# Scan of a state-space layer: making the next time steps one tile earlier, in another PSUM bank

## The reference

```python
dt = jax.nn.softplus(ts @ W_dt.T + b_dt)          # time steps, 1024 channels
A = -jnp.exp(A_log.astype(jnp.float32))
def step(state, inp):
    dt_t, B_t, C_t, u_t = inp
    dA = jnp.exp(dt_t[..., None] * A)             # 16 decays per channel
    state = state * dA + (dt_t * u_t)[..., None] * B_t[:, None, :]
    y = jnp.einsum('bdn,bn->bd', state, C_t)
    return (state, y)
...
y = ys.transpose(1, 0, 2) + x * D
```

## Time and profile before

| | us |
|---|---|
| median of 3 runs (range) | 3067.13 (3065.42 to 3069.26) |
| the profiled execution | 3064.25 |
| its span, first to last instruction | 3062.5 |
| busy PE / DVE / ACT / POOL | 2417.9 / 2037.0 / 1590.3 / 1155.5 |
| the scan of batch element 0, about | 619 to 1000 |
| the scan of batch element 1, about | 1153 to 1534 |

### The profile page before, as it was taken

The page is one execution under the profiler, slowest core; times in us unless marked ns, Lnnn a source line. Parts: engine busy times, 40 slices in busy tenths (PEclk is TensorE's granted clock), DMA queues, the critical chain, the costliest instruction groups (busy, mean ns, idle before and its releaser), DMA issues.

```text
span 3062.5 us, 36612 instructions
## 1 busy us (share of the span) xinstructions
PE 2417.9 (79%) x12216; PEld 1889.0 (62%) x12216; DVE 2037.0 (67%) x3145; ACT 1590.3 (52%) x3315; POOL 1155.5 (38%) x1016
## 2 busy tenths in 40 slices
PE   6986989768778866777889889998799998952058
PEld 4344347557667655766767678886578877842046
DVE  3834742578778457877853477885578785498884
ACT  1541640277666127766611166664276664699701
POOL 3011046142123521212356546665456764510071
PEclk9887899778889977888999999999899999965579
DMA  6123223020100120010022211111111111200011
GB/s 214 44 84 97 43 66 90 16 71 14 56 21 25 52 65 22 15 56 22 25 64 88 76 28 53 52 53 52 49 32 52 56 49 56 73 28 0 0 32 45
DMA packets 87842, 155.73 MB, mean 51 GB/s; under 512 B 8840, under 2 KB 17672, under 8 KB 87528
## 3 DMA queue, kind: packets, MB, share of 16 engines
q1 hardware_dynamic: 87656, 153.38, 16.9%
HBM read 138.21 MB, written 14.75 MB: 50 GB/s over the span
## 4 chain that ended last, share of the span: by engine, by line
PE 51%; ACT 15%; DVE 15%; issue 7%; POOL 3%; DVEq 0%; ACTq 0%; POOLq 0%
PE ps L651 45%; ACT tables L1343 5%; PE ps L665 5%; ACT m L1218 3%; DVE f_lo L1382 2%; DVE m_front L1503 1%; PE ps L790 1%; POOL w_lo L595 1%; ACT tables L1182 1%; ACT m L1192 1%; DVE f_hi L1381 1%; ACT L1218 1%; DVE loose L1485 1%; DVE stat L1397 1%; DVE m L1582 1%
## 5 line engine op out<-in xcount | busy, mean ns | idle before, releaser
L594 POOL TENSOR_SCALAR w_hi<-w_in 128x512 fp32r<-128x512 f32 x430 | 315.2, 733 | 1382.4 <-PE ps L651 802.9
L595 POOL TENSOR_TENSOR w_lo<-w_in,w_hi 128x512 fp32r<-128x512 f32 x430 | 624.7, 1453 | 35.9
L651 PE MATMUL ps<-m,tables 128*128 128x128 f32 x2048 | 301.4, 297 | 136.6 <-ACT tables L1182 135.4
L651 PE MATMUL ps<-hT_hi,w_lo 128*128 128x512 f32 x864 | 355.5, 411 | 28.5 <-DVE a L1427 11.7
L651 PEld LDWEIGHTS ps<-m,tables 128*128 128x128 f32 x2048 | 273.6, 209 | 156.0 <-issue 131.0
L651 PE MATMUL ps<-hT_hi,w_hi 128*128 128x512 f32 x864 | 342.6, 397 | 0.0
L651 PE MATMUL ps<-hT_lo,w_hi 128*128 128x512 f32 x864 | 342.2, 396 | 0.0
L1582 DVE TENSOR_TENSOR_SCAN m<-m,m 128x1028 f32<-128x1028 f32 x128 | 308.0, 2406 | 10.0 <-ACT m L1218 4.3
L1218 ACT ACTIVATE m<-m_rows,negA 128x256 f32<-128x256 f32 x512 | 217.3, 498 | 22.2 <-DVE m L1536 15.5
L1554 DVE TENSOR_TENSOR m<-m,m 128x1024 f32<-128x1024 f32 x128 | 177.6, 1388 | 55.3 <-PE ps L665 39.0
L665 PE MATMUL ps<-tables,m 128*128 128x128 f32 x1024 | 164.4, 292 | 63.1 <-DVE m L1582 39.7
(11 more groups left out here) (245 smaller groups left out, 5308.6 us busy)
## 6 DMA issues: line engine op xcount, KB each, us to landing
w_in<-units SPq DMA_DIRECT2D x430, 256.0 KB, 2.6
stack_scratch<-a SPq DMA_DIRECT2D x48, 256.0 KB
a<-stack_scratch SPq DMA_DIRECT2D x64, 192.0 KB, 4.4
m<-bc_scratch SPq DMA_DIRECT2D x16, 512.0 KB, 5.4
out<-x_sb SPq DMA_DIRECT2D x2, 1024.0 KB, 4.3
tables<-small SPq DMA_DIRECT2D x1, 1143.0 KB, 9.9
x_sb<-x SPq DMA_DIRECT2D x4, 256.0 KB, 3.6
x_sb<-x SPq DMA_DIRECT2D x1, 1024.0 KB, 7.6
```

Of the source, the lines that this page charges most:

```text
L594: c["did"](nc.gpsimd.tensor_scalar(w_hi[:, r], raw, 1.0, 1.0, ALU.mult, ALU.mult), s["unit_hi"])
L595: c["did"](nc.gpsimd.tensor_tensor(w_lo[:, r], raw, w_hi[:, r].bitcast(F32), ALU.subtract), s["unit_split"])
L651: ins = T.matmul(out, lhsT, rhs, start=start, stop=stop)
```

## The change

It does two things in the scan.

1. The time steps of tiles i + 2 and i + 3 (i even) are now started in tile i: PE makes the product ahead of the second group of the even tile, in **bank 4**, which it shares with the feed-forward's gate and projection; ACT takes Abs, Relu and Exp at the end of the even tile's second half, and Ln after the first group of the odd tile; DVE's three pieces come before the second, third and fourth group of the odd tile. The semaphore `m_dtx` now tells ACT that the steps are ready, and is raised before the product with the input.
2. The helper `at_ends` is removed, and the feed-forward parts are placed by `mix`, which puts part k after half tile number n when (n + 1) * 30 // 32 passes k.

```diff
-    def at_ends(scans, parts):
-        ...
-            want = (2 * tile + last + 1) * len(parts) // (2 * ends) if last else done + (...) // 2
-    ... + at_ends(scan(0), ffn(1, 4)[3:])
+    ... + mix(scan(0), ffn(1, 4)[3:])
-    ... + at_ends(scan(1), ffn(0, 4)[3:])
+    ... + mix(scan(1), ffn(0, 4)[3:])
@@ PE
                 def time_steps(i):
-                    o, tokens = claim(6, s["m_dt_clip"]), (half + i // DT) * HL
+                    o, tokens = claim(4, s["m_dt_clip"]), (half + i // DT) * HL
-                if q == 0 and i % 2 and (half, i) != (1, DT - 1):
-                    time_steps(i + 1)
                 for g in range(q * QS // NG, (q + 1) * QS // NG):
                     n = scan_group(b, half, i, g)
+                    if g == 1 and i % 2 == 0 and (half, i) != (1, DT - 2):
+                        time_steps(i + 2)
                     states_turned(n, 0)
@@ ACT
-                        go(A(m_e[:, r], ps[:, 6, r * HL:(r + 1) * HL], ACT.Abs, bias=bias))
+                        go(A(m_e[:, r], ps[:, 4, r * HL:(r + 1) * HL], ACT.Abs, bias=bias))
                     ...
                     did(A(m_e, m_e, ACT.Exp, scale=-1.0), s["m_dt_exp"])
+
+                def time_steps_ln():
                     did(A(m_l, m_e, ACT.Ln, bias=1.0), s["m_dt_ln"])
...
                         states_kept(n - 2, 1)
+                    if g == 0 and i % 2 and (half, i) != (1, DT - 1):
+                        time_steps_ln()
-                if q == 0 and i % 2 and (half, i) != (1, DT - 1):
-                    time_steps(i + 1)
+                if q == 1 and i % 2 == 0 and (half, i) != (1, DT - 2):
+                    time_steps(i + 2)
@@ DVE
-                    did(V.tensor_tensor(dt, dt, m_v, ALU.add))
+                    did(V.tensor_tensor(dt, dt, m_v, ALU.add), s["m_dtx"])
+
+                def time_inputs(i):
...
-                    if q == 1 and i % 2 and (half, i) != (1, DT - 1):
-                        if g == QS // NG:
+                    if i % 2 and (half, i) != (1, DT - 1):
+                        if g == 1:
                             time_steps_1(i + 1)
-                        else:
+                        elif g == 2:
                             time_steps_2(i + 1)
+                        elif g == 3:
+                            time_inputs(i + 1)
```

More of the change, by code:

```diff
@@ L131, in schedule @@
     s += flat(ffn(0)[:3]) + [("attn_out", 1), ("ln_rows", 1), ("fgate", 0, 1, 5), ("fproj", 0, 1, 5), ("fmul", 0, 1, 5), ("ln_turn", 1), ("fdown", 0, 0)]
-    s += flat(ffn(0)[6:]) + flat(ffn(1)[:2]) + ln(0) + flat(ffn(1)[2:3]) + front(0) + at_ends(scan(0), ffn(1, 4)[3:])
+    s += flat(ffn(0)[6:]) + flat(ffn(1)[:2]) + ln(0) + flat(ffn(1)[2:3]) + front(0) + mix(scan(0), ffn(1, 4)[3:])
     s += back(0)[:1] + ln(1) + back(0)[1:]
-    s += front(1) + ln(0) + flat(ffn(0)[:3]) + at_ends(scan(1), ffn(0, 4)[3:])
+    s += front(1) + ln(0) + flat(ffn(0)[:3]) + mix(scan(1), ffn(0, 4)[3:])
     s += back(1)[:1] + ln(0) + back(1)[1:]
@@ L1162, in time_steps @@
                         bias = col("b_dt", i % DT + r, i % DT + r + 1)
-                        go(A(m_e[:, r], ps[:, 6, r * HL:(r + 1) * HL], ACT.Abs, bias=bias))
-                        go(A(m_dt[:, i % 4 + r], ps[:, 6, r * HL:(r + 1) * HL], ACT.Relu, bias=bias), s["m_dt_clip"] if r else None)
+                        go(A(m_e[:, r], ps[:, 4, r * HL:(r + 1) * HL], ACT.Abs, bias=bias))
+                        go(A(m_dt[:, i % 4 + r], ps[:, 4, r * HL:(r + 1) * HL], ACT.Relu, bias=bias), s["m_dt_clip"] if r else None)
                     own(s["act_step"], 0)
                     did(A(m_e, m_e, ACT.Exp, scale=-1.0), s["m_dt_exp"])
+                def time_steps_ln():
                     did(A(m_l, m_e, ACT.Ln, bias=1.0), s["m_dt_ln"])
@@ L1533, in time_steps_2 @@
                     did(V.tensor_tensor(m_v, m_l, m_v, ALU.subtract), s["m_dt_sub"])
-                    did(V.tensor_tensor(dt, dt, m_v, ALU.add))
+                    did(V.tensor_tensor(dt, dt, m_v, ALU.add), s["m_dtx"])
+                def time_inputs(i):
+                    dt = m_dt[:, i % 4:i % 4 + 2]
                     at = (half + i // DT) * HL
-                    did(V.tensor_tensor(m_dtx, dt, m_xs[:, i % DT:i % DT + 2, at:at + HL], ALU.mult), s["m_dtx"])
+                    did(V.tensor_tensor(m_dtx, dt, m_xs[:, i % DT:i % DT + 2, at:at + HL], ALU.mult))
                 def skip():
@@ L1565, in scan @@
                         time_steps_2(0)
+                        time_inputs(0)
                         go(V.memset(m_dA[:, :, 0:1], 0.0))
```

## The result

| | before | after |
|---|---|---|
| median of 16 runs each (range) | 3069.4 us (3062.3 to 3078.0) | 3083.5 us (3070.2 to 3089.8) |
| ratio after / before | | 1.0047 (1.0032 to 1.0061) |
| span of the profiled execution | 3062.5 | 3078.0 |
| scan 0, first to last recurrence | 373.9 | 383.2 |
| scan 1 | 373.4 | 385.4 |

The change makes the kernel 0.5% slower, 14 us. Forecast were 38 us less. In the two profiles the scans are 21.3 us longer, the stretch between them and all that follows them have the same length to 0.1 us, and the first scan merely starts 5.8 us sooner. That is no part of the change: in the 14 profiles of this document the first recurrence starts anywhere between 612 and 628 us, and one VectorE instruction well ahead of it stands at 357.4 us before and at 348.5 after.

What follows compares the result with a forecast made beforehand. No engine was full; about 85 us per scan went to waits handed round PE, DVE and ACT. Pair gains and losses summed to 19 us per scan, 38 in both: 3026 against the profile, 3029 against the median, range 2978 to 3064.

Steps and rivals of the forecast that it cites:

- Part 2 costs and gives nothing.: Placement of feed-forward parts: old and new rule give an identical list of items, so no time changes.
- What goes.: At time steps, every PE-to-ACT-to-PE wait for the product disappears; PE lost about 53 us per scan to them.
- the bound of 106 us: Upper limit on the gain: PE's waits at the time steps, over both scans.
- What it wins behind the boundary: 81: From the even tile's skip term to the next even tile's second recurrence: 81.1 us won in all.
- pair 0: First tile pair of a half: 23.4 us to the skip, 24.85 behind; 48.3 against 53.5, gain 5.2.
- pair 2: Tile pair with SiLU right behind Exp: 20.6 us to the skip; 44.8 against 43.4, loss 1.4.
- pair 4: Tile pair with 24 matmuls in mid odd tile: 18.6 us to the skip; 45.1 against 48.0, gain 2.9.
- pair 6: Tiles 6 and 7: 17.5 us to the skip; 45.9 against 51.5, gain 5.6, with 3.5 for tile 8's diagonals.
- Up to the boundary the change loses 0.4 to 4.6 us in each pair.: From even tile's second recurrence to its skip's end: moved ACT work delays the skip, 43.3 us in all.
- a bare boundary of 12.05 us: Starting sum to the skip's end with nothing extra on ACT: 3 x 3.45 + 1.2 + 0.5.
- The table loads at 1.28 us.: On ACT: six further table loads (97 to 103) at 1.28 us each, without the skill's 1.38 us drain.
- The second one: Rival: boundary wait outgrows the old one; loss from skips 2.7 us later, 3085 at 4 us; chance 0.11.

Runs made afterwards that it cites:

- e4: The changed kernel with VectorE's time-step pieces back ahead of the odd tile's third and fourth group: 3150.3 us, ratio 1.0244 to the kernel before.
- e1: The changed kernel with Ln and its two table loads one group later on ScalarE, behind the even tile's fourth-group copies: 3030.1 us, ratio 0.9860.
- e9: e1 with Abs, Relu and Exp reading only 8 columns (Exp: of each half) from the third tile pair on: 3022.3 us, ratio 0.9860.
- e10: e1 with TensorE's product made only 8 columns wide from the third tile pair on: 3027.7 us, ratio 0.9892.
- e3: The kernel before with the product moved to the even tile's end, ahead of the feed-forward part, still in bank 6: 3047.3 us, ratio 0.9923.
- e12: The kernel before with ScalarE's copies of the turned states ahead of the decays in each group: 3025.0 us, ratio 0.9871.
- e6: e1 with ScalarE's copies of the turned states ahead of the decays in each group: 3030.7 us, ratio 0.9885.

## Why the prediction was wrong, step by step

- *Part 2 costs and gives nothing.* By the two lists of items, which are equal, there was nothing to measure.
- *What goes.* Right: the round trip is gone, and the bound of 106 us held, with 88.7 us won behind the boundary.
- *What it wins behind the boundary: 81.* Right, 88.7; pair 0 25.3 for 24.85, pair 2 24.5 for 24.2, pair 4 25.9 for 26.5. In pair 6, 24.2 for 28.4: the 3.5 us for the diagonals of tile 8 don't show in this leg. Two of the sums are off by 0.15 and cancel: 19.75 + 2.0 is 21.75, not 21.6, and 19.75 + 4 is 23.75, not 23.9. e4 shows where the win comes from, which the prediction put to the round trip alone: without the earlier pieces on VectorE 63 us of it are lost.
- *Up to the boundary the change loses 0.4 to 4.6 us in each pair.* This is the step that failed. Measured were 5.9 to 10.2 us, 110.4 us in all where the sum had 43.3. The mechanism was named (ScalarE's pieces ahead of the copies of the fourth group, VectorE at `skip`), its size was not. By the runs, Ln's place costs 54 us (e1); the sum has at most 14 x 3.2 = 45 for it, so it is some 9 of the missing 67. The larger part is the 57 us that e1 leaves, for which the sum has next to nothing beside Ln. Some 24 of them go with Abs to Exp (e9) and some 12 with the product in the middle of the even tile (e10), which I left out of the working to the skip because the two matmuls "stay on PE"; the waits for bank 4, 5.0 us per scan in the profile, are partly in these. Some 10 to 20 us stay unassigned, and no run prices the bank alone.
- Why it was too small: pairs 2, 4 and 6 were worked from a bare boundary of 12.05 us, where the kernel before took 13.7 to 18.3 us without any of the moved pieces. VectorE's own `fmul` was put at nothing there: in pair 4 it is 0.75 + 0.86 + 1.64 = 3.25 us of work, and it waits for the projection, so that the product and the wait for bank 4 reach the skip through it (e1). I also started pair 4 with TensorE in time. It comes out of 24 matmuls there (5.8 us), so its copies come when ScalarE is in Ln, and nothing of Ln falls in a gap. And I priced the outputs behind the new wait at the full clock, 1.8 us for the two sets; they took 3.78 [the windows above]. How much each of these makes up over all pairs is not shown. In pair 0, which was worked from the measured 18.8, the skip came 5.9 us later too than the 23.4 given.
- In pair 2 I had SiLU ready to load its table at once. In the changed kernel the load comes only when the gate's matmuls are done (the last one starts at 682.44 and takes 0.40 us), as the profile after shows for tile 2:

```profile
679.62 0.66 ACT L1155 ACTIVATE m_rows<-m_rows 128x512 f32<-128x512 f32 x1
...
682.91 1.28 ACT L1124 ACT_TABLE_LOAD   x1 [2.63 <-issue]
684.21 0.69 ACT L1124 ACTIVATE loose<-ps,tables 128x512 f32<-128x512 f32 x1
```

- *The table loads at 1.28 us.* The row held, six more loads in all and no pause of its own behind a load; the drain of "ScalarE: Activation LUTs", What ACT_TABLE_LOAD costs, in the Trainium skill is in no run here (SiLU starts 1.30 us after its load again, 682.91 to 684.21).
- *The rivals.* The second one happened, at the point that it named: the skips come 4.8 us later than worked out (67.1 / 14), where 2.7 was the turn. Its sign came too: pair 4 loses, 51.5 us from second recurrence to second recurrence against 48.0. It had 0.11. That 3083 was measured and 3085 named for 4 us is in part luck: by its own arithmetic 4.8 us give 14 x 2.1 = 29 us slower, and 7.6 us more than forecast were won behind the boundary. The profile gave reason for more: VectorE's skips already waited for TensorE in two of the four pairs before, so what was put ahead of those had no slack to fall into.

## What to carry to other kernels

When work is moved out of a round trip, price it at its new place against the tightest hand-over that follows it there, not against the engine's average idle time: ScalarE was idle for some 30% of the scan, and still 3.2 us of Ln cost 3.8 us each time, until one digit put it behind the copies. Start such a working from the measured length of the stretch, with the waits and the other work that are in it, and not from a bare one. Doing the producer's part sooner (e3) was safe here, since it put hardly anything ahead of a boundary; doing the consumer's part sooner was not. And where two things are due on an engine at the same event, the one that another engine stands still for goes first: the copies ahead of the decays gave 1.3% on the kernel before (e12), though nothing on e1 (e6).

## What the runs showed of the hardware

- In the changed kernel TensorE's granted clock falls within its idle stretch of 3.5 us (0.79 over it), is 0.50, 1.2 GHz, in the 4.0 us behind, and the next 16 output matmuls take 3.78 us instead of e1's 2.05. There the new wait cost its own length and about 1.7 us more. That isn't a price for every wait: over the scans as a whole the granted clock is 0.87 before, 0.89 after, and 0.90 and 0.92 in e1.
- The same instructions can meet the slow clock in one scan and not in the other. In e1 the same product takes 2.07 us in scan 0 (granted clock 0.50 from 673.30 to 675.40) and 1.12 us in scan 1 (1.00 from 1194.60 to 1195.80), and pair 2 is 22.1 us to the skip there and 18.9 here. The whole of a scan differs by 4.2 us (360.0 and 355.8) for it and for what else moves. From e1's timeline of TensorE, scan 0 and scan 1:

```profile
673.34 2.07 PE L640 MATMUL ps<-tables 32*128 32x256 f32 x4
...
1194.64 1.12 PE L640 MATMUL ps<-tables 32*128 32x256 f32 x4
```

- A table load is on the path or not by where it falls next to a wait. In pair 2 of the changed kernel SiLU's load starts 0.07 us after the gate's last matmul ends, and SiLU 1.30 us behind it (682.91 and 684.21 above). In the kernel before the load ran ahead of the wait for the same matmuls, and cost nothing. What decides between the two is not shown. The kernel before, tile 2:

```profile
684.60 1.28 ACT L1135 ACT_TABLE_LOAD   x1
688.12 0.69 ACT L1135 ACTIVATE loose<-ps,tables 128x512 f32<-128x512 f32 x1 [2.24 <-PE ps L651]
```
